# Writing out all 38 steps of a software-pipelined conv + FFN kernel instead of looping over pairs of images

## What is computed

```python
x = x + _L0_conv_ref(_ln_c(x), 0)            # 3x3 mean filter per channel
t = _to_tokens(x)
t = t + _L0_ffn_ref(_ln_t(t), L0_ffn_Wa, L0_ffn_ba, L0_ffn_Ws, L0_ffn_bs)
x = _from_tokens(t, x)
# _L0_ffn_ref: out = x; a decoded nibble pair, an opcode pair and three marks per token
y_add = _pipeline(x_ge, Wa, ba)              # three layers, relu after two
y_sub = _pipeline(x_ge, Ws, bs)
out = out.at[..., OUTPUT_LO:OUTPUT_LO + 16].add(2.0 * oh_lo)
out = out.at[..., OUTPUT_HI:OUTPUT_HI + 16].add(2.0 * oh_hi)
out = out.at[..., CARRY].add(carry)
```

## Time and profile before

| | us |
|---|---|
| median of 3 runs | 665.66 (665.02 to 668.44) |
| profiled execution, its own time | 666.22 |
| its span, first to last instruction | 664.2 |
| DVE busy | 543.3 (82%) |
| ACT busy | 497.0 (75%) |
| PE busy | 485.5 (73%) |
| POOL busy | 264.2 (40%) |
| granted TensorE clock, mean | 0.936 |

### The profile page before, as it was taken

How to read it: one execution, slowest core, us unless ns; L and a number is a source line. 1 busy time by engine, 2 the same in 40 slices (tenths; PEclk the granted TensorE clock), 3 DMA queues, 4 the chain that set the end, 5 groups by cost and what they waited for, 6 DMA issues and landing times.

```text
span 664.2 us, 10610 instructions
## 1 busy us (share of the span) xinstructions
PE 485.5 (73%) x2262; PEld 201.9 (30%) x2294; DVE 543.3 (82%) x1506; ACT 497.0 (75%) x707; POOL 264.2 (40%) x580
## 2 busy tenths in 40 slices
PE   0034568889888888878788888878788888887760
PEld 0011223333333333323333333323333333433220
DVE  1478989999999999969999999788999999875120
ACT  0001689888888888868889988868888888988740
POOL 0022444444444444424444444433444444452100
PEclk9997779998999998979999998979999999999895
DMA  9999940099269939996569944910559079393999
GB/s 175 198 191 199 199 68 0 10 177 193 34 97 144 183 56 128 114 165 104 64 96 169 179 60 66 176 17 0 64 72 118 1 83 76 42 86 40 87 88 73
DMA packets 592754, 67.96 MB, mean 102 GB/s; under 512 B 592568, under 2 KB 592696, under 8 KB 592696
## 3 DMA queue, kind: packets, MB, share of 16 engines
q1 hardware_dynamic: 591696, 67.30, 81.9%
q10 hardware_dynamic: 1000, 0.11, 0.1%
HBM read 33.84 MB, written 33.55 MB: 101 GB/s over the span
## 4 chain that ended last, share of the span: by engine, by line
DVE 31%; PE 23%; issue 22%; ACT 13%; DVEq 3%; SPq 3%; POOL 2%; ACTq 1%; DMA 1%; POOLq 0%
DVE n L543 13%; PE ps L877 8%; PE ps L846 6%; ACT xbuf L754 6%; DVE stat L553 5%; DVE xbuf L571 4%; PE ps L900 3%; ACT h L774 3%; SPq L293 3%; PE ps L882 3%; ACT h L766 2%; POOL nlo L653 1%; PE ps L894 1%; ACT featT L791 1%; PE ps L891 1%
## 5 line engine op out<-in xcount | busy, mean ns | idle before, releaser
L754 ACT ACTIVATE xbuf<-xbuf,shift,gain (+1 forms) x256 | 225.0, 934 | 0.0
L653 POOL TENSOR_TENSOR nlo<-n,nhi 128x1024 f16<-128x1024 f32 x64 | 137.5, 2149 | 165.0 <-ACT nhi L798 164.9
L877 PE MATMUL ps<-h,w2m 128*128 128x512 f32 x256 | 140.8, 633 | 79.5 <-ACT featT L791 73.7
L553 DVE BATCH_NORM_STATS2 stat<-xbuf 128x6 f32 (+1 forms) x256 | 171.4, 686 | 21.1 <-DMA xbuf<-x 21.1
L543 DVE SCALAR_TENSOR_TENSOR n<-xbuf,stat,ps 128x256 f32<-128x256 f32 x256 | 153.9, 657 | 0.1
L846 PE MATMUL ps<-nhi,band 128*128 128x512 f16 (+1 forms) x408 | 111.7, 389 | 27.3 <-POOL nlo L653 26.2
L571 DVE TENSOR_TENSOR xbuf<-ps,xbuf 128x512 f32 (+1 forms) x128 | 91.8, 717 | 33.0 <-PE ps L846 18.0
L798 ACT ACTIVATE nhi<-n 128x1024 f16<-128x1024 f32 x64 | 67.6, 1056 | 55.3 <-DVE n L543 50.7
L846 PE MATMUL ps<-nlo,band 128*128 128x512 f16 (+1 forms) x408 | 107.4, 377 | 0.0
L774 ACT ACTIVATE h<-ps,b2m 128x512 f32<-128x512 f32 x128 | 87.5, 684 | 17.7 <-PE ps L877 17.6
L766 ACT ACTIVATE h<-ps 128x512 f32<-128x512 f32 x128 | 75.2, 587 | 22.9 <-remote 16.7
(11 more groups left out here) (87 smaller groups left out, 495.3 us busy)
## 6 DMA issues: line engine op xcount, KB each, us to landing
xbuf<-x SPq DMA_DIRECT2D x32, 512.0 KB, 6.8
xbuf<-x SPq DMA_DIRECT2D x16, 1024.0 KB, 10.5
out<-xbuf SPq DMA_DIRECT2D x32, 512.0 KB, 7.2
out<-xbuf SPq DMA_DIRECT2D x12, 1024.0 KB, 12.8
out<-xbuf SPq DMA_DIRECT2D x16, 256.0 KB, 8.4
consts<-cst SPq DMA_DIRECT2D x1, 176.0 KB, 2.4
h<-ws ACTq DMA_DIRECT2D x4, 0.2 KB
b2r<-bs ACTq DMA_DIRECT2D x4, 0.1 KB
```

Source lines behind the costliest of these rows:

```text
L553: return v.bn_stats(stat[:, j % 4, at + 2 * s:at + 2 * s + 2, :].rearrange("p w n -> p (w n)"), xview(par)[:, w:w + 2, :].rearrange("p w c ...
L653: pool.tensor_tensor(nlo[:, at:at + HALF, :], n32[:, h, :, :], nhi[:, at:at + HALF, :], ALU.subtract).then_inc(lo_ready, 1)
L754: ins = act.activation(col, col, ACT.Identity, bias=shift[:, k, w:w + 1], scale=gain[:, k, w:w + 1])
L877: pe.matmul(ps[:, B_L2, :], w2m[:, :], h1[:, slot(i, jc), :], start=True, stop=True).then_inc(l2_done, 1)
```

## The change

`run_steps` issues all 38 steps with constants; the loop of three passes is gone on DVE, ACT, POOL and PE. SP's program is unchanged. All lines behind L133 move up by 9 (L458 becomes L449, L571 becomes L562, L900 becomes L891 and so on).

```diff
 def run_steps(eng, step):
 
-    for t in range(CHUNKS):
-        step(t, t, 0)
-    with eng.Fori(1, PAIRS) as pair:
-        for j in range(CHUNKS):
-
-            with eng.register(f"pair_{eng.engine.name}_{j}") as copy:
-                eng.reg_mov(copy, pair)
-                here = eng.snap(copy, min_val=1, max_val=PAIRS - 1)
-                step(here * CHUNKS + j, j, here)
-    for t in range(NCHUNK, LAST_STEP):
+    for t in range(LAST_STEP):
         step(t, t % CHUNKS, t // CHUNKS)
```

## The result

| | before | after |
|---|---|---|
| median, us | 665.34 (664.76 to 668.44) | 645.67 (644.0 to 647.4) |
| ratio | | 0.9701, 95% interval 0.9667 to 0.9735 |
| profiled execution, own time and span, us | 666.22, 664.2 | 647.4, 645.6 |

The forecast was 645.7 us. The median before stands here over four executions, the three of the table ahead of the prediction and one more.

A forecast was written before the change was run, and what follows sets the result against it. DVE was taken to bound the kernel, all but filling each 17.25 us looped step. Savings of 10.0 + 0.6 + 8.6 + 1.05 + 0.2 = 20.5 us from 666.2 gave 645.7 us; range 640 to 656.5.

The forecast's parts named there:

- The two turns: DVE steps where the loop branches back: without waiting for code after the jump, 4.35 and 5.65 us saved, together 10.0.
- the clock: Step behind the second turn, 1.2 us long at a granted clock of 0.87: half counted as gain, 0.6 us.
- Rival B: Gaps at the turns are something else and stay; only the register part pays, 656.3 us; chance 0.04.
- The register part: Looped steps, between DVE's mark and decoding: dropping register instructions saves 0.36 us a step over 24 steps, 8.6 us.
- 1.05 + 0.2 for longer steps: Three looped steps with a further issue gap ahead of L483 save 1.05 us; a few steps of 17.33 another 0.2.
- wait ahead of L460: DVE in the profile after: L460 13.3 us behind the mark, with a wait for PE L891 in most steps.
- Code at nothing: Eight-step body fetched as straight code three times over instead of jumped back to: costed at nothing.
- more packets on the instruction queue: Sign expected in the profile after: the instruction queue carries more packets, with no new issue gap on DVE, ACT or PE.
- Rival D: Code comes late over the queues that move x, stalling DVE 4.8 us each; six stalls give 674.5 us; chance 0.05.
- Start and end: Steps 0 to 7 and 32 to 37 and SP's program, same in both kernels: 0 us gained or lost.
- A: Only the turns pay; DVE's shorter gaps return as a longer wait for PE L900: 655.6 us; chance 0.08.
- C: PE's and ACT's chain shrinks too, all DVE gaps go, 17.0 us in place of 8.6: 637.3 us; chance 0.06.

The follow-up runs named there:

- registers_straight: Kernel before, with steps 8 to 31 as straight code on DVE, ACT and PE, register instructions kept, POOL still looped: 655.25 us, ratio 0.9837.
- near_jump: Kernel after, plus a two-pass DVE loop of four memsets at the head of steps 16 and 24: 647.58 us, ratio 0.9712.
- turn_sizes: Kernel after, plus nine three-pass DVE loops of 64 to 640 memsets behind the last step: run once, 936.3 us.
- results_later: Kernel after, with DVE taking the result's first operation and the next one place later: 645.5 us, ratio to before 0.9677.
- only_pe_looped: Kernel before, with DVE, ACT and POOL written out and only PE keeping its loop: 646.43 us, ratio 0.9705.
- The fills: Kernel after plus extra matmuls in PE's idle stretch each step: seven, 642.67 us; with the result's operations one place later, seven 633.04 us, three 632.92 us.

## Why the prediction was right

**The two turns, 10.0 us.** Right in cause and size. The steps that held them took 21.60 and 22.90 us and take 17.92 and 16.92 now; the first of them happens to hold a half-clock stretch. With the registers kept and only the jumps gone the kernel took 655.25 us, 10.1 us under the median before, where the sum had 10.0, or 10.6 with the clock. Against the executions of the kernel before that were run beside it, the ratio of 0.9837 makes it 10.9 us, with an interval from 7 to 15. That it was code, and not the load or the head of the pair, was argued in the prediction; registers_straight, near_jump, turn_sizes and the packets in its gaps show it. Rival B asked that the two gaps stay, and they are gone; a turn of a few instructions does cost little, 0.34 us with its wait in near_jump.

**The register part, 8.6 us, and 1.05 + 0.2 for longer steps.** Right. Plain steps take 16.83 to 16.96 us (the last of the middle 16.57); 16.89 was forecast from steps 5 and 7. The wait ahead of L460 grew from 0.26 to 0.48 us as forecast, since L891 ends 13.2 us behind the mark. That this wait is the cap was shown by results_later: moved out of the way, the step is 16.6 us. The steps with the extra gap ahead of L483 are now plain ones. From registers_straight to after there are 9.6 us, where the sum had 9.85. One thing was left open in the text and is settled now: the registers that matter are DVE's; PE's cost nothing that shows, with only_pe_looped at 646.43 us, and ACT's 0.1 us a step at most.

**The clock, 0.6 us.** This term was mis-sized. The guess was that half of the 1.2 us after the second turn would go. All of it went, but the middle now holds five steps with a half-clock stretch, at 17.8 to 18.0 us. Before, it held three at 18.0 to 18.1, the one of 18.46 after the second turn, and one that the prediction did not count, the last step, which takes 16.57 us in the kernel after:

```profile
560.47:577.98 17.51, 15.55 (x73) 6.67 (x74) 15.49 (x45) 15.31 (x23) 8.25 (x18) 0.90 0.39 31
```

Of the difference, 17.51 - 16.57 - 0.36 = 0.6 us is not the registers' and goes to the clock. Counted against plain steps the clock costs 5.1 us after and 3 x 0.8 + 1.2 + 0.6 = 4.2 before: the term had the wrong sign, by 1.5 us in all, which is most of the way from the 20.5 us of the sum to the middle's 19.2. The middle's mean clock still rose, from 0.96 to 0.98. Two of the seven half-clock stretches before lasted 6.8 us instead of 3.4 and began at 289.3 and 432.7 us, while PE stood idle for 4.0 and 3.8 us behind a turn. The first of them cost next to nothing: the step behind that turn took 17.36 us. This counts one execution of each kernel; the four of the kernel after have a mean clock from 0.942 to 0.955, and the profiled one is the lowest. What sets the number of such stretches the prediction left open, though PE's idle time stood in the same profile. The fills show that work put into that idle time removes them.

**Code at nothing.** Right: no "issue" gap on DVE in the middle. The point "more packets on the instruction queue" was wrong. The rows of queues 14 and 8 on the page after:

```profile
q8 instruction: 19, 0.31, 0.2%
q14 instruction: 30, 0.25, 0.1%
```

That is 0.56 MB; before it was 0.39 + 0.16 = 0.55 MB. In the middle alone it is 0.41 MB in both, though the body is passed three times in one kernel and stands there three times in the other. So the loop fetched its body anew in each pass, and written-out code moves no more bytes. Rival D let code come over the same queues as x; on both pages code has queues 14 and 8 and x has queue 1.

**Start and end, 0.** Off by 1.0 and -0.4 us, of which 0.6 us is a longer wait for the first load of x (21.7 against 21.1 us).

**The rivals.** A asked that the saved time come back ahead of L460: 0.22 us of some 0.45 a step did, which was in the forecast; the rest did not. C, all gaps gone, did not come of itself; the results taken one place later bring its step of 16.6 us, and then the clock takes it. D did not happen on any engine. That two misses, the clock and the start, are made good in the medians by the spread of single executions (644.0 to 647.4 us) is luck; the terms are right to about 1 or 2 us, not to the 0.03 by which the total agrees.

## What to carry to other kernels

Look for idle time called "issue" on the busiest engine at the top of its loop: a jump back over a body of 384 instructions or more cost DVE 2.9 to 6.4 us, one over a body of up to 320 no more than 0.5, and register work for waits and addresses showed where it stood behind a wait for the engine's own last instruction. Price the written-out form from steps of the same program that are already written out, and name the wait that caps the gain. And when a step gets shorter but the time does not, compare the steps' clock before anything else.

## What the runs showed of the hardware

In turn_sizes a turn of DVE's loop costs 0.3 to 0.5 us up to 320 instructions and 2.9 us or more from 384 on, with a peak of 6.2 to 6.4 us at 384. In straight code of memsets of some 28 ns each, DVE pauses 0.30 to 0.35 us after every 128 of them, with one packet of 8 KB on queue 14 for each such piece; in the second and third pass through a body of up to 320 there is neither a pause nor a packet. Nothing of that is seen between the kernel's own, longer instructions.

With PE idle once in each step for 2.2 us, the granted clock fell in five of the 24 steps of the kernel after, and in eight of 24 when the step was shortened by 0.3 us; with three matmuls in that stretch, 1.8 us of it still idle, it fell in none. A half-clock stretch cost 1.0 us in the kernel after and 1.35 us with the results one place later. There DVE no longer had its wait for PE's small matmuls, which could hide a part; that this is the reason was not tested.
